# Edge steps of a two-layer graph kernel: GpSimd adds the bias to a group's x between the two halves of the next group's gathers

## What is computed

```python
def layer0(x, adj, weight, bias, node_w, edge_w):
    node_att = softmax(x @ node_w, axis=0)
    h = x @ edge_w
    e = where(adj > 0, h @ h.T, NEG_BIG)
    combined_att = node_att * softmax(e, axis=1)
    return adj * combined_att @ (x @ weight) + bias

h = maximum(layernorm(x), 0)
x = x + layer0(h, adj, ...)          # the edge steps compute this
h = maximum(layernorm(x), 0)
x = x + layer1(h, adj, W)            # a second stage, not touched
```

## Time and profile before

| what | value |
|---|---|
| runs, us | 710.37, 711.59, 720.1 |
| the profiled execution's own time, us | 714.95 |
| its span, first to last instruction, us | 713.2 |
| mean granted clock of TensorE, share of full | 0.856 |
| PE busy | 495.1 us, 69% of the span |
| DVE busy | 478.2 us, 67% |
| POOL busy | 388.6 us, 54% |
| ACT busy | 351.1 us, 49% |
| the edge steps | about 90 to 456 us of the span |

### The profile page before, as it was taken

One profiled execution on the slowest core, in us unless ns is written; L12 is line 12 of the kernel. 1 busy time (PEld: TensorE's weight loads), 2 busy tenths in 40 slices (PEclk: granted clock), 3 DMA queues, 4 the chain that ended last, 5 costly groups with the idle time before them and its releaser, 6 DMA issues.

```text
span 713.2 us, 12464 instructions
## 1 busy us (share of the span) xinstructions
PE 495.1 (69%) x3804; PEld 416.4 (58%) x3804; DVE 478.2 (67%) x1977; ACT 351.1 (49%) x718; POOL 388.6 (54%) x458
## 2 busy tenths in 40 slices
PE   3697573749688777967877877987267587665750
PEld 2476442638688666866776767876245465544540
DVE  3486868887878768776887667777524354466774
ACT  2597765655564755526431465386412122234454
POOL 4053527274671736647575730038277777777752
PEclk9889866959999896978979899999669889999995
DMA  8955599986768886786232320001543334335632
GB/s 303 397 199 185 170 370 382 346 314 213 294 218 304 287 312 227 257 324 216 79 95 72 104 61 1 1 1 57 190 106 105 105 104 103 108 107 134 197 96 91
DMA packets 38166, 129.00 MB, mean 181 GB/s; under 512 B 6224, under 2 KB 23504, under 8 KB 34000
## 3 DMA queue, kind: packets, MB, share of 16 engines
q1 hardware_dynamic: 22736, 84.87, 31.5%
q0 software_dynamic: 15360, 43.29, 22.1%
HBM read 115.49 MB, written 12.65 MB: 180 GB/s over the span
## 4 chain that ended last, share of the span: by engine, by line
PE 28%; DVE 23%; POOL 16%; issue 12%; ACT 7%; DVEq 5%; DMA 5%; SPq 2%; POOLq 1%; ACTq 1%
POOL work L1486 10%; PE bank L815 10%; POOL work L709 5%; PE bank L754 3%; DVE fs L1049 3%; PE bank L864 3%; DMA work<-table_h,work 2%; PE bank L786 2%; PE bank L240 2%; PE bank L1768 2%; DMA table_h<-front 2%; PE bank L1585 2%; DVEq L1204 2%; DVE gx L1537 1%; DVE front L1066 1%
## 5 line engine op out<-in xcount | busy, mean ns | idle before, releaser
L709 POOL DMA_INDIRECT work<-table_h,work x160 | 160.0, 1000 | 74.1 <-issue 67.2
L609 ACT ACTIVATE work<-work 128x2048 bf16<-128x2048 f32 x64 | 121.8, 1903 | 59.6 <-issue 23.7
L1486 POOL DMA_INDIRECT work<-table_y,idx x128 | 124.3, 971 | 39.0 <-issue 38.1
L815 PE MATMUL bank<-work 128*128 128x128 f32 x640 | 102.6, 327 | 19.2 <-DVEq L1095 19.2
L815 PEld LDWEIGHTS bank<-work 128*128 128x128 f32 x640 | 96.6, 239 | 21.1 <-DVEq L1095 18.5
L1585 PE MATMUL bank<-work 128*128 128x257 f32 x256 | 75.5, 446 | 36.1 <-DMA work<-table_y,idx 36.0
L1585 PEld LDWEIGHTS bank<-work 128*128 128x128 f32 x256 | 53.8, 219 | 55.3 <-DMA work<-table_y,idx 47.1
L754 PE MATMUL bank<-work 128*128 128x256 bf16 x512 | 69.6, 292 | 0.0
L1049 DVE CUSTOM_DVE_ANT_0 fs<-work,bank 128x256 f32<-128x256 f32 x160 | 56.4, 417 | 11.8 <-DMA work<-table_h,work 6.1
L1614 ACT ACTIVATE work<-bank 128x257 f32<-128x257 f32 x32 | 12.2, 382 | 100.9 <-PE bank L1585 100.9
L1351 DVE SCALAR_TENSOR_TENSOR fs<-work 128x256 f32<-128x256 f32 x32 | 13.6, 426 | 71.2 <-ACTq L1615 70.6
(11 more groups left out here) (271 smaller groups left out, 1017.6 us busy)
## 6 DMA issues: line engine op xcount, KB each, us to landing
work<-in_adj SPq DMA_DIRECT2D x32, 2048.0 KB, 9.6
table_y<-work SPq DMA_DIRECT2D x8, 520.0 KB, 4.3
gx<-in_x SPq DMA_DIRECT2D x8, 512.0 KB, 8.5
table_h<-front SPq DMA_DIRECT2D x8, 512.0 KB, 4.4
front<-in_x POOLq DMA_DIRECT2D x8, 512.0 KB, 6.9
out<-gx SPq DMA_DIRECT2D x8, 512.0 KB, 3.2
work<-table_h,work POOLq DMA_INDIRECT x160, 3.6
work<-table_y,idx POOLq DMA_INDIRECT x128, 2.8
```

The costliest lines, as they stand in the source:

```text
L609: a.activation(abf[:, u % HALVES, :], adu[:, b % 2, h, :], ACT.Copy, accum_out=cnt[:, k, b, h:h + 1]).then_inc(L["conv"], 1)
L709: p.indirect_dma_start(gat[:, k, n, :], None, table_h, bass.IndirectOffsetOnAxis(ix[:, k, n:n + 1], 0)) \
L815: last = t.matmul(bank[4 + b % 2][:, c * P:(c + 1) * P], gat[:, k, n, c * P:(c + 1) * P], otp[:, n, :], start=(q == 0), stop=(q == TILES - 1))
L1486: p.indirect_dma_start(gtm[:, n % OCT, q, :], None, table_y, bass.IndirectOffsetOnAxis(idx[:, n * TILES + q:n * TILES + q + 1], 0)) \
```

## The change

One function changes. In a step POOL first issued all 20 gathers of `ls`, then the load of x of the same group, waited for it and added the bias. Now it issues the first 10 gathers of `ls`, then waits for x of `at_`, the group of the step before, and adds the bias to that, then issues the last 10 gathers of `ls`, and at last the load of x of `ls`, for which it no longer waits in this step. The semaphores and their counts are the same; so is every instruction's size.

```diff
         def fast_pool(p):
+            def gather(g, k, first, last):
+                for n in range(first, last):
+                    p.indirect_dma_start(gat[:, k, n, :], None, table_h,
+                                         bass.IndirectOffsetOnAxis(ix[:, k, n:n + 1], 0)) \
+                        .then_inc(L["gat"][k][n // TILES], 16)
+
             def body(wd, ls, at_, ag_):
                 if ls:
                     g, k = ls
                     p.wait_ge(L["agg"], GB * g + 2)
                     p.wait_ge(L["idx"], g + 1)
                     p.sem_inc(s_go, 1)
-                    for n in range(GT):
-                        if n == GT // 2:
-                            p.wait_ge(L["agg"], GB * g + GB)
-                            p.sem_inc(s_go, 1)
-                        p.indirect_dma_start(gat[:, k, n, :], None, table_h,
-                                             bass.IndirectOffsetOnAxis(ix[:, k, n:n + 1], 0)) \
-                            .then_inc(L["gat"][k][n // TILES], 16)
-                    p.wait_ge(L["x1"], GB * g + GB)
-                    p.dma_start(xr2[:, k, :, :], x_r[:, grp(g), :]).then_inc(L["x"], 16)
+                    gather(g, k, 0, GT // 2)
+                if at_:
+                    g, k = at_
                     p.wait_ge(L["x"], 16 * (g + 1))
                     for b in range(GB):
                         p.tensor_tensor(xr2[:, k, b, :], xr2[:, k, b, :], bias_bc[:, :], ALU.add)
                     p.drain().then_inc(L["xb"], 1)
+                if ls:
+                    g, k = ls
+                    p.wait_ge(L["agg"], GB * g + GB)
+                    p.sem_inc(s_go, 1)
+                    gather(g, k, GT // 2, GT)
+                    p.wait_ge(L["x1"], GB * g + GB)
+                    p.dma_start(xr2[:, k, :, :], x_r[:, grp(g), :]).then_inc(L["x"], 16)
             staged(p, body, 1)
```

## The result

The changed kernel is slower: 714.4 us, the median of 20 runs (711.87 to 719.57), against 710.58 us for 20 runs of the kernel before (705.98 to 720.1). The ratio is 1.0064, with a 95% interval of 1.0043 to 1.0085; it leaves out the run of 720.1 us, which lies over 1.5% above the fastest of its kernel. The forecast was 706.4 us and a range of 698 to 713.

A forecast was written before the change was run, and what follows sets the result against it. DVE and PE handing work to each other bound the kernel, POOL beside them. Stretch terms -1.5 + 0.2 + 1.1 - 2.0 - 4.6 + 1.6 gave -5.2 us: 711.6 to 706.4 us, range 698 to 713.

The forecast's parts named there:

- D: Stretch from group 3's first dot to group 4's: 3.35 us wait gone, by_slot hit +1.7, edge_list -0.3; -2.0 us.
- E: Stretch from group 4's first dot to group 5's: 2.80 us wait gone, 1.8 more taken back, by_slot already hit; -4.6 us.
- the 1.8 us of PE's clock: In E: the excess of 44.4 over 42.6 us, with the lowest granted clock, 0.82, would go with the wait.
- A: Stretch from group 0's first dot to group 1's: additions leave by_slot, -1.7, may touch edge_list, +0.2; -1.5 us.
- B: Stretch from group 1's first dot to group 2's: by_slot hit costs 1.7 us instead of 1.4 to 1.5; +0.2 us.
- The collision: POOL's additions fall beside DVE's by_slot in every full step, lengthening it from 2.49 to 4.21 us, +1.7 us.
- C: Stretch from group 2's first dot to group 3's: by_slot hit +1.7, edge_list freed -0.6; +1.1 us.
- F: Stretch from group 5's first dot to group 6's: by_slot hit entered as +1.6 us, nothing else.
- The slower one: Rival: hits on by_slot cost the additions' whole length, 2.79 us a step, giving 712.1 us; chance 0.10.
- the clock of E not coming back: Within the slower rival: E's lower clock stays as well as 2.79 us hits, giving 713.9 us.
- the late gathers: Rival: second-half gathers land later than 9.4 us, dots wait as before, about 714 us; chance 0.07.
- The additions miss by_slot: Rival: additions do not fall on by_slot in B to F, so no hits there, about 698 us; chance 0.17.

The follow-up runs named there:

- the second profile of before: Kernel before, unchanged, profiled again: span 705.9 us, execution 707.61 us; timed ratio of the kernel to itself 1.0034, median 713.15 us.
- the first profile: Kernel before, unchanged, the profile the prediction was made from, also called the earlier trace: that execution took 714.95 us.

## Why the prediction was wrong

*What bounds the kernel.* Right in kind: DVE and PE hand work round, POOL runs beside them, and late gathers cost only where a dot waits. Wrong in what the profile stood for. The step that failed is the sum's reference: the terms of D and E, -3.35 and -2.80 with the 1.8 us of PE's clock, 7.95 us together, belong to one execution. The other two profiles of before have 0 and 2.93 us of dot waits, none of them in D or E, and steps of 41.0 there. The prediction took the difference off the median, 711.6, but what only that execution had to give back cannot be taken off a median.

The side of the changed kernel came out much better. The stretches of the earlier trace rows with the prediction's terms make 40.0, 41.8, 42.0, 42.2, 42.6, 40.8 and 33.8 us, 283.2 in all; measured were 41.1, 40.7, 42.3, 43.9, 43.4, 40.4 and 33.5, 285.3 in all. So 2.1 us of the miss lie there, most of them in D.

*The hits before.* The same error a second time. A, B and E were entered as already hit by the additions, for -1.5, +0.2 and 0. In the second profile of before by_slot is hit nowhere. There POOL waits 4 to 6 us for x and the additions lie beside dots and keys; in the first profile it waited 8 to 13 us in groups 1 to 4, and they slid onto by_slot and edge_list, and the next gathers toward the dots. Against the second profile the changed kernel's edge steps end 8.3 us later (454.0 against 445.7). The forecast's own +1.7 in five stretches, 8.5 us, comes near that by luck: four stretches were hit, for 6.1 us, and most of the rest is what D and E took beyond their hits. The medians of the timed runs lie only 3.8 us apart. How often an execution of before is like its first profile and how often like its second is not known from three, so the 3.8 are not derived here. That a late landing of x is what tells the executions apart fits the three profiles; the run with x loaded earlier did not show it clearly.

*The collision.* Right in place and nearly in size: 1.53 us a step (2.49 to 4.02) where 1.7 was taken, in C to F. Not in B, where the additions came at 181.6, when the last operation of by_slot was running; that one kept its 1.16 us. The rule of the Trainium skill (SBUF — State Buffer, Who interferes with whom) agrees with what was measured on both sides: the tensor_tensor with two inputs in SBUF, L1070, took 0.71 us beside an addition and 0.17 alone, and the dots with one input in PSUM took the same time beside the additions as without them (ten of them 3.6 us, from 221.8 to 225.4 with the additions from 221.5 to 224.3, in the run with seven gathers ahead; 3.6 us, from 216.6 to 220.2, in the changed kernel with hardly any beside them). A cast with a single input, L1071, was hit as well, 0.60 us against 0.20; no run shows in which port mode it ran.

*What a hit costs in all.* Mis-sized. C to F are 7.8 us longer than with the wait for by_slot (1.2, 2.9, 2.2 and 1.5), and the hits sum to 6.1. The rest lies in D and E. In D the late sums took 7.21 us against 6.34 at the same place of the second profile of before and of the run with the wait for by_slot; the granted clock of that stretch was 0.84 against 0.88 in both. PE had idled 3.20 us for by_slot ahead of them, against 1.85 and 1.66. But it had idled 3.20 us in C too, where the sums took 6.26 at a clock of 0.88, so the idle time alone does not explain D.

```profile
268.22 7.21 PE L822 MATMUL bank<-work 128*128 128x128 f32 x40
```

```profile
265.12 6.34 PE L815 MATMUL bank<-work 128*128 128x128 f32 x40
```

In E the clock was 0.88 and the stretch still 2.2 us longer than with the wait for by_slot, a hit and 0.7 us more; that part is not settled.

*The gathers.* Right in the main: from group 3 on they start about 1 us behind the index (group 2's 3.4 us, behind the gathers of group 1, which POOL's stall had made late), the second half of groups 3 to 6 at the end of the late sums, and no dot waited, though the landings were slower than in the rows used: 5.8 us in the median and 10.5 at most, against 3.6 and 9.4. It bought little, since in two of the three profiles of before no dot waited beyond stretch B, and the waits in B stay possible, since POOL's stall comes in either order.

*The load of x.* Right that it is hidden, also in stretch A; only the last group's additions, with no gathers ahead of them, waited 3.96 us for it.

*The rivals.* The slower one had the right direction, but by another step: it needed a hit of 2.7 us a step, and the hit was 1.53. It set this point of decision against gains of 10.3 us that were those of one execution. Against the second profile of before there is next to no gain, and nearly any hit decides. Two cases that the prediction itself worked out, the collision with the clock of E not coming back (713.9) and the late gathers (714), stood above its range's end of 713. The measured 714.4 lies near both by luck: no dot waited, and the hit was not 2.79. "The additions miss by_slot" is what the wait for by_slot made: 707.8 us, where 698 was worked out with the same gains of one execution. Smaller slips change nothing: F's collision, priced at 1.7, was entered as 1.6, and the twenty gathers of group 3 took 26.0 us in the earlier trace rows, not 25.9.

*Behind the edge steps.* The prediction put nothing there. From the last new x to the end took 260.0 us in the profile after and 256.7 in the first of before, and that 3.3 us is why the pair of profiles shows a longer span in spite of shorter edge steps (714.0 against 713.2):

```profile
454.00:714.00 260.00, 160.03 (x816) 125.22 (x814) 147.79 (x548) 103.06 (x248) 164.51 (x176) 0.85 0.36 103
```

```profile
445.70:705.90 260.20, 165.59 (x816) 129.30 (x814) 147.46 (x548) 102.96 (x248) 164.80 (x176) 0.82 0.36 103
```

The second profile of before has 260.2 too, so it is not the change. Over 14 profiles it was 256.7 once, 257.7 or 257.8 in three, and 259.7 to 260.3 in ten; what chooses was not looked for.

## What to carry to other kernels

Before a gain is taken out of waits in one profile, ask whether the same kernel's other executions have them: here the profiled one took 714.95 us against a median of 710.6, and its waits were the very ones that the forecast gave back. An instruction of GpSimd that is moved off a wait lands beside something else on DVE, and if, as here, index, dots and gathers keep their distances, it lands there step after step. In this kernel the dots and the key search, with an input in PSUM, were the free places, and one wait for the end of by_slot was enough to get there. The change only moved 2.8 us of work a step, and its place was worth some 6 us in all.

## What was not expected of the hardware

- A wait added ahead of GpSimd's additions made the kernel some 6 us faster (medians 714.4 and 707.8 us).
- Three of DVE's operations, of 20 to 64 elements, took 0.60 to 0.71 us each beside GpSimd's additions of 0.70 us, and 0.17 to 0.23 us alone: about the length of an addition, whatever their own size. An operation of 960 elements took 1.16 us alone and 1.55 beside the additions (at 385.94 us, in the run with seven gathers ahead).
- GpSimd stands still once for 7.7 to 10.5 us ahead of its first addition, and for 8.9 us in the changed kernel without additions. Where a dot waited behind it, in four profiles, stretch B took 44 to 48 us, not 41; in two of them the additions fell on by_slot as well.
- Between a row of additions and the next gather GpSimd paused 2.65 to 2.69 us each time in the kernel before; between a gather and the additions behind it, not at all (218.85 + 0.95 to 219.83).
